# Transposing the attention probabilities as f32 products into both banks of the scores

## The chip, the cores and the metric

The kernel runs on one core of a Trainium2 chip. The metric is the device time of one execution in microseconds. The kernel before takes 629.36 us, the median of three runs (629.0 to 629.54). All times in the sections below come from one profiled execution of it, with 629.1 us and a span of 627.3 us from its first to its last instruction.

## The reference

One layer of a transformer in f32: 16 sequences of 256 tokens with 256 features. Attention has 16 query heads and 4 key and value heads of 128, and a mask that leaves each query the first 4 keys and the last 32. Then follows a feed-forward step whose input and weight are quantised to int8.

```python
x = L0_attn_x                                              # (16, 256, 256)
x = x + attn(layernorm(x), wq, wk, wv, wo)
x = x + ffn(layernorm(x), weight, bias)

# attn
q = (x @ wq.T).reshape(b, t, 16, 128).transpose(0, 2, 1, 3)
k, v = ...                                                  # 4 heads, each used by 4 query heads
scores = einsum('bhtd,bhsd->bhts', q, k_full) / sqrt(128)
mask = (k <= q) & ((k < 4) | (k >= q - 32 + 1))
attn = softmax(scores where mask)
out = einsum('bhts,bhsd->bhtd', attn, v_full) ... @ wo.T

# ffn
w_q, x_q = int8 rounding by row maxima / 127
y = (x_q @ w_q.T) * x_scale * w_scale + bias
```

## The kernel before

The work is cut into 64 units, unit u being batch u // 4 and key head u % 4 with its four query heads. To hold f32 precision with f16 operands, each factor is a high and a low f16 half, and each product is three matmuls (PAIRS). A sequence of 256 queries is cut into 9 steps of 28 or 32 queries with 64 keys each, so a unit's probabilities are PP, 9 tiles of 128 rows (4 heads x 32 queries) by 128 columns (64 keys, high and low half).

The order on each engine is written out by hand, as one loop over turns t = 1 to 60 after a start, and a tail for the last three units. Turn t on TensorE: scores of unit t, PV of unit t - 2 (lines 563 and 564), q fill of unit t + 1 (line 446), a k fill (line 413) or v fill (line 422) for the next batch, then one of these: x's transposes (t mod 4 = 3, line 401), the transposes of quantised x (t mod 4 = 1, line 612), the FFN product (t mod 4 = 2, line 627); then the transposes of the probabilities of unit t - 1 (line 534), and the output projection of unit t - 2 (line 581).

ScalarE in a turn: p_high (line 850), o_high twice (857), q_high (814), exps (821), q_high again, k_high (800 and 801) or v_high (809), x's copy (825) or quantised x's copy (837), and the copy of the transposed probabilities PT (pt_evac, line 830). VectorE: s_max (991, 993), o_low (1007), q_low (983), probs (998 to 1002), q_low, k_low (973) or v_low (978), then by t mod 4 the FFN's steps, among them ffn_norm (1028), and ln_stats (957, 959) of a later batch at t mod 4 = 0. GpSimd: p_low (1320), s_shift (1306), p_norm (1314), and ln_rstd (1288, 1290) at the end of a turn with t mod 4 = 0, ahead of the next turn's p_low. Engines wait for one another by semaphores that count: pt_ok counts the copies of PT, s_m the s_max steps.

PSUM has 8 banks. The scores of a unit lie in banks 2 and 3 (BANK_S). Bank 2 (BANK_PT) also takes the transposed probabilities, as f16 in half of it at a time, and bank 3 (BANK_F) takes x's and quantised x's transposes and the FFN product.

Of the kernel before, what the change touches and what calls it, by code (L numbers as in the profile page):

```python
# [6 lines left out]
F16 = mybir.dt.float16  # L7
# [3 lines left out]
ACT = mybir.ActivationFunctionType  # L11
AX = mybir.AxisListType

B, T, D = 16, 256, 256
# [49 lines left out]
def build(nc, x_d, wq_d, wk_d, wv_d, wo_d, wf_d, bias_d, mask_d, idh_d, idb_d, idf_d, out_d):  # L64
    with ExitStack() as ctx:
# [76 lines left out]
        def half(i, dt):  # L142
            return banks[i].bitcast(dt)
# [125 lines left out]
        def pt_bank(u):  # L269

            return BANK_KV if u in (NU - 4, NU - 3, NU - 1) else BANK_PT
# [72 lines left out]
        def _(pe):  # L344
# [47 lines left out]
            def x_transpose(b):  # L392

                pe.wait_ge(ln_l, b + 1)
                if b:
                    pe.wait_ge(s_m, 1 if b == 1 else 4 * (b - 1))
                v = half(BANK_F, F16).rearrange("p (k l t) -> p k l t", k=2, l=2)
                for k in range(2):
                    for l in range(2):
                        for t in range(2):  # L400
                            a = pe.transpose(v[:, k, l, t * 128:t * 128 + 128], xhl[:, t, l, k * 128:k * 128 + 128], idh[:, :])  # L401
                a.then_inc(xt_ps, 1)
# [94 lines left out]
            def kv_fill(t):  # L497

                b, g = divmod(t, KV)
                if t == 0:  # L500
                    pe.wait_ge(v_l, 1)
                    k_fill(0, 1)
                elif t == 1:
                    pe.wait_ge(xt_ok, 2)
                    pe.wait_ge(k_l, 2)
                    k_fill(1, 0)
                elif t == 2:
                    pe.wait_ge(k_l, 3)
                    v_fill(1, 0)

                    pe.wait_ge(s_m, t + 1)
                    v_fill(1, 1)
                else:
                    if g == 0:
                        pe.wait_ge(xt_ok, b + 2)
                    pe.wait_ge(k_l if g < 2 else v_l, 2 * b + (2, 3, 3, 4)[g])
                    kind, n = KV_TILE[g]
                    (v_fill if kind else k_fill)(b + 1, n)

            def p_transpose(u):  # L520
                p = u % 2
                pe.wait_ge(p_l, u + 1)

                if u == NU - 4:
                    pe.wait_ge(k_l, 2 * B)
                elif u == NU - 3:
                    pe.wait_ge(pt_ok, u)
                elif u == NU - 1:
                    pe.wait_ge(pt_ok, u - 1)
                else:  # L530
                    pe.wait_ge(s_m, u + 2)
                v = half(pt_bank(u), F16).rearrange("p (h q) -> p h q", h=4)
                for s in reversed(range(NT)):
                    a = pe.transpose(v[:, :, STEP * s:STEP * s + 32], PP[:, p, s].rearrange("p l k -> p (l k)"), idh[:, :])  # L534
                a.then_inc(pt_ps, 1)

            def pv(u, j):
                b, g = divmod(u, KV)
                if j == 0:
                    pe.wait_ge(pt_ok, u + 1)  # L540
                    if g == 0 and b < 2:
                        pe.wait_ge(z_ok, 1) if b == 0 else pe.wait_ge(ld_z, 16)
                if g == 0:
                    pe.wait_ge(vw2[j][b % 2], 16 * (b // 2 + 1))
                if u == NU - 3:

                    pe.wait_ge(q_l, 2 * (NU - 1) + j + 1)
                elif u > NU - 3:

                    pe.wait_ge(o_l, 2 * u + j - 3)  # L550
                    if u == NU - 2 and j == 0:
                        pe.wait_ge(f_y, 2 * (B - 2))
                elif u:

                    pe.wait_ge(o_l, 2 * u + j - 1)
                elif j == 0:

                    pe.wait_ge(w_l, l_at("q3"))
                for s, c0, c1 in output_pieces(j):
                    w = max(s - 1, 0)  # L560
                    o = banks[o_bank(u, j)][:, :].rearrange("p (h q) -> p h q", h=4)[:, :, c0 - 128 * j:c1 - 128 * j]
                    pt = PT[:, u % 2].rearrange("p (h q) -> p h q", h=4)[:, :, c0:c1]
                    pe.matmul(o, VW[b % 2][:, w, 0, g * 128:g * 128 + 128], pt, start=True, stop=False)  # L563
                    a = pe.matmul(o, VW[b % 2][:, w, 1, g * 128:g * 128 + 128], pt, start=False, stop=True)  # L564
                a.then_inc(o_ps, 1)
# [36 lines left out]
            def ffn_t(b):  # L602

                pe.wait_ge(f_xq, b + 1)
                if b == B - 2:

                    pe.wait_ge(pt_ok, NU - 1)
                else:
                    pe.wait_ge(s_m, 4 * b + 10)
                for t in range(2):  # L610
                    for k in range(2):
                        a = pe.transpose(xq_view(b, t)[:, k, :], xq[:, t, k * 128:k * 128 + 128], idb[:, :])
                a.then_inc(ft_ps, 1)

            def ffn_mm(b):
                pe.wait_ge(f_t, b + 1)
                if b == 0:
                    pe.wait_ge(wf_s, 14)
                if b < B - 3:

                    pe.wait_ge(s_m, 4 * b + 11)
                elif b == B - 3:

                    pe.wait_ge(o_l, 2 * (NU - 4) + 1)
                for t in range(2):
                    for k in range(2):
                        a = pe.matmul(fm_view(b, t), xqT[:, k, t * 128:t * 128 + 128], WfT[:, k, :], start=(k == 0), stop=(k == 1))  # L627
                a.then_inc(fm_ps, 1)
# [18 lines left out]
            def ffn_weights():  # L647
                v = half(BANK_F, BF16)[:, 0:512].rearrange("p (k o) -> p k o", k=2)
                pe.wait_ge(wf_s, 12)
                pe.wait_ge(ld_idb, 16)  # L650

                pe.wait_ge(s_m, 9)
                for k in range(2):
                    for t in range(2):
                        a = pe.transpose(v[:, k, t * 128:t * 128 + 128], wfi[:, t, k * 128:k * 128 + 128], idb[:, :])
                a.then_inc(wf_ps, 1)

                pe.wait_ge(q_l, 2 * 9 + 1)
                pe.matmul(banks[0][:, 0:256], ones[:, :], diag[:, :, :].rearrange("p t o -> p (t o)"),
                          start=True, stop=True).then_inc(wf_ps, 1)  # L660
# [38 lines left out]
            for t in range(1, NU - 3):  # L699
                b, g = divmod(t, KV)  # L700
                back, more = t > 1, b + 1 < B
                last, mm = at(9, t), at(10, t)
                scores(t)
                if back:
                    pv(t - 2, 0)
                    pv(t - 2, 1)
                q_fill(t + 1, 0)
                q_fill(t + 1, 1)
                if t == 1:
                    columns_up("o")  # L710

                    pe.wait_ge(w_l, l_at("q2"))
                    pe.wait_ge(ld_q[3], 16)
                    w_transpose("q3", big[:, 3, :])
                    maxima_out("o")
                if more:
                    kv_fill(t)
                if g == 3 and b + 2 < B:
                    x_transpose(b + 2)
                if t == 8:  # L720
                    ffn_weights()
                if last is not None:
                    ffn_t(last)
                if mm is not None:
                    ffn_mm(mm)
                p_transpose(t - 1)
                if back:
                    if t == 2:

                        pe.wait_ge(w_s, s_at("o"))  # L730
                    out_proj(t - 2)
                if 1 <= t <= 4:
                    wo_transpose(t - 1)
# [43 lines left out]
        def _(act):  # L777
# [49 lines left out]

            def pt_evac(u):
                act.wait_ge(pt_ps, u + 1)
                act.activation(PT[:, u % 2], half(pt_bank(u), F16), ACT.Copy).then_inc(pt_ok, 1)  # L830

            def ffn_t_evac(b):
                act.wait_ge(ft_ps, b + 1)
# [53 lines left out]
            for t in range(1, NU - 3):  # L887
# [8 lines left out]
                q_high(t + 1, 1)  # L896
                if t == 1:
                    w_high("q3")
                if t == 1:
                    k_high(1, 0)  # L900
                elif t == 2:
                    v_high(1, 0)
                    v_high(1, 1)
                elif more:
                    kind, n = KV_TILE[g]
                    (v_high if kind else k_high)(b + 1, n)
                if g == 3 and b + 2 < B:
                    x_evac(b + 2)
                if last is not None:
                    ffn_t_evac(last)  # L910
                pt_evac(t - 1)
                if t == 2 or (g == 1 and t > 1 and b + 2 < B):
                    ln_split(b + 2)
                if 1 <= t <= 4:
# [520 lines left out]
```

## Time and profile before

| | |
|---|---|
| median of 3 runs | 629.36 us (629.0 to 629.54) |
| profiled execution | 629.1 us, span 627.3 us |
| TensorE busy | 599.1 us, 96% |
| VectorE busy | 542.1 us, 86% |
| ScalarE busy | 399.7 us, 64% |
| GpSimd busy | 314.3 us, 50% |
| mean granted TensorE clock | 0.988 |

TensorE is busy nearly all the time. Its instructions overlap: a matmul's row lasts from its start to its last result, so the cost of a run of matmuls on the engine is read from the start of the run to the start of what follows it. The same holds, by some 0.1 us, for rows of ScalarE and VectorE. PE is TensorE, PEld its weight loads, DVE VectorE, ACT ScalarE, POOL GpSimd.

### The profile page before, as it was taken

The numbers are of one execution on the slowest core, as the hardware profiler recorded it, in microseconds if no ns is written. First come the engines' busy times: TensorE is split into PE (matmuls) and PEld (weight loads), VectorE is DVE, ScalarE is ACT, GpSimd is POOL, SyncE is SP. The second block draws the span as 40 slices with busy tenths as digits, with TensorE's granted clock in tenths as the row PEclk, the third lists the DMA queues.
The fourth block names the chain that finished last, engine by engine and source line by source line (L and its number), as shares of the span: only waits on it lengthen the run. The fifth ranks groups of instructions, "written<-read, shape, count | busy, mean of one in ns | idle before, by whom it ended". The sixth has DMA issues, their size and how long they took to land.

```text
span 627.3 us, 18165 instructions
## 1 busy us (share of the span) xinstructions
PE 599.1 (96%) x7589; PEld 528.9 (84%) x7589; DVE 542.1 (86%) x1083; ACT 399.7 (64%) x632; POOL 314.3 (50%) x310
## 2 busy tenths in 40 slices
PE   5759999999999999999999999999999999999994
PEld 4547888889898888989898898989888898988883
DVE  5876899989888998989898897989899898889886
ACT  5676766566766666667666666766666667666670
POOL 1132445454555646456554645556464545546463
PEclk9989999999999999999999999999999999999997
DMA  8940401213040221304031120304012130402101
GB/s 293 356 108 19 118 1 45 60 28 93 2 119 2 70 51 37 84 6 114 2 93 29 44 77 11 110 2 113 9 51 70 26 95 3 118 2 73 47 12 41
DMA packets 33841, 41.31 MB, mean 66 GB/s; under 512 B 3936, under 2 KB 24416, under 8 KB 33760
## 3 DMA queue, kind: packets, MB, share of 16 engines
q1 hardware_dynamic: 33616, 40.02, 23.0%
q8 instruction: 60, 0.98, 0.7%
q14 instruction: 21, 0.17, 0.1%
q10 hardware_dynamic: 144, 0.13, 0.1%
HBM read 10.26 MB, written 4.19 MB: 23 GB/s over the span
## 4 chain that ended last, share of the span: by engine, by line
PE 88%; DVE 6%; ACT 2%; issue 2%; POOL 1%; DMA 1%; POOLq 0%; SPq 0%; DVEq 0%; ACTq 0%
PE ps L446 25%; PE ps L581 25%; PE ps L476 7%; PE ps L413 7%; PE ps L422 6%; PE ps L534 5%; PE ps L564 4%; PE ps L563 4%; PE ps L401 1%; PE ps L627 1%; PE ps L353 1%; DVE WoT L1121 1%; DMA small<-in_L_attn_wk 1%; PE ps L596 1%; DVE Qs L983 1%
## 5 line engine op out<-in xcount | busy, mean ns | idle before, releaser
L446 PE MATMUL ps<-xT,WqT 128*128 128x256 f16 x1536 | 178.3, 273 | 2.0 <-DVE WqT L1121 1.3
L581 PE MATMUL ps<-WoT,pool 128*128 128x256 f16 x1440 | 167.3, 273 | 0.2 <-DVE pool L1007 0.2
L446 PEld LDWEIGHTS ps<-xT,WqT 128*128 128x128 f16 x1536 | 146.9, 98 | 19.0 <-issue 3.0
L581 PEld LDWEIGHTS ps<-WoT,pool 128*128 128x128 f16 x1440 | 138.2, 98 | 15.3 <-DVE pool L1007 0.3
L1314 POOL TENSOR_TENSOR small<-E,rr 128x576 f32<-128x576 f32 x64 | 73.7, 1152 | 98.4 <-DVE rr L1002 98.4
L857 ACT ACTIVATE pool<-ps 128x512 f16<-128x512 f32 x128 | 69.6, 595 | 81.5 <-PE ps L564 81.4
L1320 POOL TENSOR_TENSOR PP<-small,PP 128x576 f16<-128x576 f32 x64 | 82.2, 1284 | 68.2 <-ACT PP L850 68.2
L814 ACT ACTIVATE Qs<-ps 128x576 f16<-128x576 f32 x128 | 82.5, 644 | 44.9 <-PE ps L446 44.9
L1306 POOL TENSOR_TENSOR Sm<-Sm,mx 128x576 f32<-128x576 f32 x64 | 73.7, 1152 | 53.8 <-DVE mx L993 52.4
L983 DVE TENSOR_TENSOR Qs<-ps,Qs 128x576 f16<-128x576 f32 x128 | 92.6, 724 | 4.7 <-ACT Qs L814 4.7
L1007 DVE SCALAR_TENSOR_TENSOR pool<-ps,pool 128x512 f16<-128x512 f32 x128 | 81.8, 680 | 0.0
L991 DVE TENSOR_TENSOR Sm<-ps,mask 128x576 f32<-128x576 f32 x64 | 47.7, 745 | 27.5 <-PE ps L476 27.5
L830 ACT ACTIVATE PT<-ps 128x1024 f16<-128x1024 f16 x64 | 66.0, 1032 | 6.1 <-PE ps L534 6.1
L821 ACT ACTIVATE E<-Sm,esc 128x576 f32<-128x576 f32 x64 | 49.6, 775 | 28.7 <-POOL Sm L1306 28.7
L998 DVE TENSOR_REDUCE sm<-E 128x9 f32<-128x576 f32 x64 | 48.0, 751 | 18.0 <-ACT E L821 18.0
L476 PE MATMUL ps<-Kw,Qs 128*128 128x64 f16 x1728 | 61.0, 193 | 2.5 <-ACT xT L825 1.4
L476 PEld LDWEIGHTS ps<-Kw,Qs 128*128 128x128 f16 x1728 | 58.7, 98 | 5.2 <-ACT xT L825 1.5
L993 DVE TENSOR_REDUCE mx<-Sm 128x9 f32<-128x576 f32 x64 | 48.2, 754 | 2.2
L413 PE MATMUL ps<-xT,WkT 128*128 128x256 f16 x384 | 49.5, 281 | 0.0
L422 PE MATMUL ps<-WvT,xT 128*128 128x512 f16 x192 | 46.5, 379 | 0.0
L850 ACT ACTIVATE PP<-small 128x576 f16<-128x576 f32 x64 | 43.9, 685 | 2.1 <-POOL small L1314 2.0
L413 PEld LDWEIGHTS ps<-xT,WkT 128*128 128x128 f16 x384 | 38.7, 101 | 5.4
(129 smaller groups left out, 910.3 us busy)
## 6 DMA issues: line engine op xcount, KB each, us to landing
VW<-Vn SPq DMA_DIRECT2D x48, 120.0 KB
big<-Vn SPq DMA_DIRECT2D x48, 120.0 KB
X<-in_L_attn_x SPq DMA_DIRECT2D x16, 256.0 KB, 7.7
VW<-VW SPq DMA_DIRECT2D x16, 256.0 KB, 3.3
big<-big SPq DMA_DIRECT2D x16, 256.0 KB, 3.4
out<-pool SPq DMA_DIRECT2D x15, 256.0 KB, 3.6
big<-in_L_attn_wq SPq DMA_DIRECT2D x4, 512.0 KB, 7.9
pool<-in_L_attn_wo SPq DMA_DIRECT2D x4, 512.0 KB, 9.0
```

Source lines behind the costliest of these rows:

```text
L413: a = pe.matmul(banks[k_bank(b, f)][:, j * 256:j * 256 + 256], WkT[:, k, wl, g * 128:g * 128 + 128], xT[:, b % 2, k, xl, :], start=(n == 1 ...
L422: a = pe.matmul(banks[v_bank(b, t)][:, :], xT[:, b % 2, k, xl, t * 128:t * 128 + 128], WvT[:, k, wl, :], start=(n == 1), stop=(n == 6))
L446: a = pe.matmul(banks[BANK_Q[f]][:, j * 256:j * 256 + 256], WqT[:, k, wl, h * 128:h * 128 + 128], xT[:, b % 2, k, xl, :], start=(n == 1), ...
L476: a = pe.matmul(banks[BANK_S[c]][:, (s - s0) * KEYS:(s - s0 + 1) * KEYS], Qs[:, p, ql, s * 128:s * 128 + 128], Kw[:, b % 2, g, kl, w, :], ...
L581: a = pe.matmul(out_view(b, t), OT[:, p, ol, h, t * 128:t * 128 + 128], WoT[:, 4 * g + h, wl, :], start=first, stop=(end and g == KV - 1), ...
L814: act.activation(dst[0], src, ACT.Copy).then_inc(q_h, 1)
L857: act.activation(OT[:, u % 2, 0, :, cols], src, ACT.Copy, scale=1.0 / P_UP).then_inc(o_h, 1)
L983: dve.tensor_tensor(dst[1], src, dst[0], ALU.subtract).then_inc(q_l, 1)
L1007: dve.scalar_tensor_tensor(OT[:, u % 2, 1, :, cols], src, 1.0 / P_UP, OT[:, u % 2, 0, :, cols], ALU.mult, ALU.subtract).then_inc(o_l, 1)
L1306: pool.tensor_tensor(Sm[:, p], Sm[:, p], mx[:, p, :].unsqueeze(2).to_broadcast([128, NT, KEYS]), ALU.subtract).then_inc(s_d, 1)
L1314: pool.tensor_tensor(Pn[:, p], E[:, p], rr[:, p, :].unsqueeze(2).to_broadcast([128, NT, KEYS]), ALU.mult).then_inc(p_n, 1)
L1320: pool.tensor_tensor(PP[:, p, :, 1, :], Pn[:, p], PP[:, p, :, 0, :], ALU.subtract).then_inc(p_l, 1)
```

## The change

The probabilities of units 0 to 59 are no longer transposed by 9 PE transposes of 128 columns to f16, but by 10 ordinary products with columns of the identity, which write f32: 128 columns for the first piece, 48 and 64 where a step crosses the middle of the sequence, and 112 (4 heads x 28 queries) otherwise. The result takes 1024 f32 columns, that is both banks of the scores. ScalarE's copy reads both banks, and PT is laid out half by half instead of head by head.

Since bank 3 now holds the transposed probabilities too, the order changes: on TensorE the probabilities come right after the q fill, ahead of the k or v fill, and x's transposes, quantised x's transposes, the FFN product and a v fill of the start follow them and wait for pt_ok in place of s_m. On ScalarE the copy of PT comes right after the second q_high. The four last units keep the old form.

```diff
@@ -393,7 +393,7 @@
 
                 pe.wait_ge(ln_l, b + 1)
                 if b:
-                    pe.wait_ge(s_m, 1 if b == 1 else 4 * (b - 1))
+                    pe.wait_ge(s_m, 1) if b == 1 else pe.wait_ge(pt_ok, 4 * (b - 1) - 1)
                 v = half(BANK_F, F16).rearrange("p (k l t) -> p k l t", k=2, l=2)
                 for k in range(2):
                     for l in range(2):
@@ -508,7 +508,7 @@
                     pe.wait_ge(k_l, 3)
                     v_fill(1, 0)
 
-                    pe.wait_ge(s_m, t + 1)
+                    pe.wait_ge(pt_ok, t)
                     v_fill(1, 1)
                 else:
                     if g == 0:
@@ -529,6 +529,17 @@
                     pe.wait_ge(pt_ok, u - 1)
                 else:
                     pe.wait_ge(s_m, u + 2)
+                if u < NU - 4:
+
+                    eye = idh[:, :].rearrange("p (h q) -> p h q", h=4)
+                    for j in range(2):
+                        v = banks[BANK_S[j]][:, :].rearrange("p (h q) -> p h q", h=4)
+                        for s, c0, c1 in output_pieces(j):
+                            i = c0 - STEP * s
+                            a = pe.matmul(v[:, :, c0 - 128 * j:c1 - 128 * j], PP[:, p, s].rearrange("p l k -> p (l k)"),
+                                          eye[:, :, i:i + c1 - c0], start=True, stop=True)
+                    a.then_inc(pt_ps, 1)
+                    return
                 v = half(pt_bank(u), F16).rearrange("p (h q) -> p h q", h=4)
                 for s in reversed(range(NT)):
                     a = pe.transpose(v[:, :, STEP * s:STEP * s + 32], PP[:, p, s].rearrange("p l k -> p (l k)"), idh[:, :])
@@ -559,7 +570,7 @@
                 for s, c0, c1 in output_pieces(j):
                     w = max(s - 1, 0)
                     o = banks[o_bank(u, j)][:, :].rearrange("p (h q) -> p h q", h=4)[:, :, c0 - 128 * j:c1 - 128 * j]
-                    pt = PT[:, u % 2].rearrange("p (h q) -> p h q", h=4)[:, :, c0:c1]
+                    pt = PT[:, u % 2, 512 * j:512 * j + 512].rearrange("p (h q) -> p h q", h=4)[:, :, c0 - 128 * j:c1 - 128 * j]
                     pe.matmul(o, VW[b % 2][:, w, 0, g * 128:g * 128 + 128], pt, start=True, stop=False)
                     a = pe.matmul(o, VW[b % 2][:, w, 1, g * 128:g * 128 + 128], pt, start=False, stop=True)
                 a.then_inc(o_ps, 1)
@@ -605,8 +616,10 @@
                 if b == B - 2:
 
                     pe.wait_ge(pt_ok, NU - 1)
+                elif b == B - 3:
+                    pe.wait_ge(s_m, 4 * b + 10)
                 else:
-                    pe.wait_ge(s_m, 4 * b + 10)
+                    pe.wait_ge(pt_ok, 4 * b + 9)
                 for t in range(2):
                     for k in range(2):
                         a = pe.transpose(xq_view(b, t)[:, k, :], xq[:, t, k * 128:k * 128 + 128], idb[:, :])
@@ -618,7 +631,7 @@
                     pe.wait_ge(wf_s, 14)
                 if b < B - 3:
 
-                    pe.wait_ge(s_m, 4 * b + 11)
+                    pe.wait_ge(pt_ok, 4 * b + 10)
                 elif b == B - 3:
 
                     pe.wait_ge(o_l, 2 * (NU - 4) + 1)
@@ -649,7 +662,7 @@
                 pe.wait_ge(wf_s, 12)
                 pe.wait_ge(ld_idb, 16)
 
-                pe.wait_ge(s_m, 9)
+                pe.wait_ge(pt_ok, 8)
                 for k in range(2):
                     for t in range(2):
                         a = pe.transpose(v[:, k, t * 128:t * 128 + 128], wfi[:, t, k * 128:k * 128 + 128], idb[:, :])
@@ -713,6 +726,7 @@
                     pe.wait_ge(ld_q[3], 16)
                     w_transpose("q3", big[:, 3, :])
                     maxima_out("o")
+                p_transpose(t - 1)
                 if more:
                     kv_fill(t)
                 if g == 3 and b + 2 < B:
@@ -723,7 +737,6 @@
                     ffn_t(last)
                 if mm is not None:
                     ffn_mm(mm)
-                p_transpose(t - 1)
                 if back:
                     if t == 2:
 
@@ -827,7 +840,11 @@
 
             def pt_evac(u):
                 act.wait_ge(pt_ps, u + 1)
-                act.activation(PT[:, u % 2], half(pt_bank(u), F16), ACT.Copy).then_inc(pt_ok, 1)
+                if u < NU - 4:
+                    src = ps[:, BANK_S[0]:BANK_S[1] + 1, :].rearrange("p j (h q) -> p j h q", h=4)
+                else:
+                    src = half(pt_bank(u), F16).rearrange("p (h j q) -> p j h q", h=4, j=2)
+                act.activation(PT[:, u % 2].rearrange("p (j h q) -> p j h q", j=2, h=4), src, ACT.Copy).then_inc(pt_ok, 1)
 
             def ffn_t_evac(b):
                 act.wait_ge(ft_ps, b + 1)
@@ -896,6 +913,7 @@
                 q_high(t + 1, 1)
                 if t == 1:
                     w_high("q3")
+                pt_evac(t - 1)
                 if t == 1:
                     k_high(1, 0)
                 elif t == 2:
@@ -908,7 +926,6 @@
                     x_evac(b + 2)
                 if last is not None:
                     ffn_t_evac(last)
-                pt_evac(t - 1)
                 if t == 2 or (g == 1 and t > 1 and b + 2 < B):
                     ln_split(b + 2)
                 if 1 <= t <= 4:
```

On TensorE, turn 9 (t mod 4 = 1) of the kernel before, from the q fill to the output projection. xq is quantised x, xT x transposed; the brackets name the semaphores that a row waits for.

```order
L446 MATMUL ps<-xT,WqT 128x256 [waits wf_s,q_l]
L446 MATMUL ps<-xT,WqT 128x256 x11
L446 MATMUL ps<-xT,WqT 128x256 [waits q_l]
L446 MATMUL ps<-xT,WqT 128x256 x11
L422 MATMUL ps<-WvT,xT 128x512 [waits k_l]
L422 MATMUL ps<-WvT,xT 128x512 x5
L612 MATMUL ps<-idb,xq 128x128 [waits s_m,f_xq]
L612 MATMUL ps<-idb,xq 128x128 x3
L534 MATMUL ps<-idh,PP 128x4x32 [waits s_m,p_l]
L534 MATMUL ps<-idh,PP 128x4x32 x8
L581 MATMUL ps<-WoT,pool 128x256 [waits o_l]
```

The same turn on TensorE in the changed kernel, where line 539 holds the new products, 625 quantised x's transposes and 592 the output projection.

```order
L446 MATMUL ps<-xT,WqT 128x256 x11
L539 MATMUL ps<-idh,PP 128x4x32 [waits s_m,p_l]
L539 MATMUL ps<-idh,PP 128x4x28 x3
L539 MATMUL ps<-idh,PP 128x4x12
L539 MATMUL ps<-idh,PP 128x4x16
L539 MATMUL ps<-idh,PP 128x4x28 x4
L422 MATMUL ps<-WvT,xT 128x512 [waits k_l]
L422 MATMUL ps<-WvT,xT 128x512 x5
L625 MATMUL ps<-idb,xq 128x128 [waits pt_ok,f_xq]
L625 MATMUL ps<-idb,xq 128x128 x3
L592 MATMUL ps<-WoT,pool 128x256 [waits o_l]
```

The probabilities have moved ahead of the v fill, and quantised x's transposes behind them, now with a wait for the copy of PT.

On ScalarE, the same turn before, from exps to p_high of the next turn.

```order
L821 ACTIVATE E<-Sm,esc 128x576 [waits s_d]
L814 ACTIVATE Qs<-ps 128x2x9x32 [waits q_ps]
L809 ACTIVATE Vn<-ps 128x512 [waits vw10,vw00,v_ps]
L837 ACTIVATE xqT<-ps 128x512 [waits ft_ps]
L830 ACTIVATE PT<-ps 128x1024 [waits pt_ps]
L795 ACTIVATE xhl<-xn 128x2x256 [waits xt_ps,ln_xn]
L850 ACTIVATE PP<-small 128x9x64 [waits pt_ps,p_n]
```

And now:

```order
L834 ACTIVATE E<-Sm,esc 128x576 [waits s_d]
L827 ACTIVATE Qs<-ps 128x2x9x32 [waits q_ps]
L847 ACTIVATE PT<-ps 128x1024 [waits pt_ps]
L822 ACTIVATE Vn<-ps 128x512 [waits vw10,vw00,v_ps]
L854 ACTIVATE xqT<-ps 128x512 [waits ft_ps]
L808 ACTIVATE xhl<-xn 128x2x256 [waits xt_ps,ln_xn]
L867 ACTIVATE PP<-small 128x9x64 [waits pt_ps,p_n]
```

The copy of PT has moved from behind quantised x's copy to right behind the second q_high. VectorE's and GpSimd's orders are unchanged.

## Rows read from the trace of the kernel before

**Rows 1.** The page, busy us, share of the span and instructions.
```profile
PE 599.1 (96%) x7589; PEld 528.9 (84%) x7589; DVE 542.1 (86%) x1083; ACT 399.7 (64%) x632; POOL 314.3 (50%) x310
```

**Rows 2.** Stretches: busy us and count of each engine, granted clock, DMA share, GB/s.
```profile
40.00:50.00 10.00, 5.24 (x38) 4.24 (x36) 4.75 (x13) 4.12 (x9) 3.53 (x3) 0.66 0.35 91
...
200.00:500.00 300.00, 300.00 (x3912) 267.19 (x3910) 265.48 (x524) 195.15 (x308) 163.47 (x159) 1.00 0.20 51
```

**Rows 3.** TensorE's timeline: start us, us, line, operation, tiles; turns 31 to 34.
```profile
319.31 2.78 PE L446 MATMUL ps<-xT,WqT 128*128 128x256 f16 x24
...
331.12 1.47 PE L413 MATMUL ps<-xT,WkT 128*128 128x256 f16 x12
...
337.25 2.78 PE L446 MATMUL ps<-xT,WqT 128*128 128x256 f16 x24
339.87 1.46 PE L422 MATMUL ps<-WvT,xT 128*128 128x512 f16 x6
341.17 0.39 PE L612 MATMUL ps<-idb,xq 128*128 128x128 bf16 x4
341.39 0.67 PE L534 MATMUL ps<-idh,PP 128*128 128x128 f16 x9
341.89 2.78 PE L581 MATMUL ps<-WoT,pool 128*128 128x256 f16 x24
344.51 0.95 PE L476 MATMUL ps<-Kw,Qs 128*128 128x64 f16 x27
...
345.30 0.22 PE L563 MATMUL ps<-PT,VW 128*128 128x128 f16 x1
...
346.21 2.02 PE L446 MATMUL ps<-xT,WqT 128*128 128x256 f16 x17
```

**Rows 4.** ScalarE's timeline: exps in three turns, and what follows it.
```profile
321.41 0.78 ACT L821 ACTIVATE E<-Sm,esc 128x576 f32<-128x576 f32 x1
...
331.21 0.78 ACT L821 ACTIVATE E<-Sm,esc 128x576 f32<-128x576 f32 x1 [0.54 <-POOL Sm L1306]
...
340.54 0.78 ACT L821 ACTIVATE E<-Sm,esc 128x576 f32<-128x576 f32 x1 [1.13 <-POOL Sm L1306]
341.22 0.63 ACT L814 ACTIVATE Qs<-ps 128x576 f16<-128x576 f32 x1
341.75 0.58 ACT L809 ACTIVATE Vn<-ps 128x512 f16<-128x512 f32 x1
```

**Rows 5.** Timelines near 50 us: a copy of PT, and the matmul that it releases.
```profile
49.93 1.03 ACT L830 ACTIVATE PT<-ps 128x1024 f16<-128x1024 f16 x1
...
51.10 0.95 PE L476 MATMUL ps<-Kw,Qs 128*128 128x64 f16 x27 [0.61 <-ACT PT L830]
```

**Rows 6.** ScalarE's timeline: k_high in a turn with t mod 4 = 0.
```profile
332.63 0.97 ACT L800 ACTIVATE Kw<-ps 128x960 f16<-128x960 f32 x1
333.50 0.22 ACT L801 ACTIVATE Kw<-ps 128x64 f16<-128x64 f32 x1
```

**Rows 7.** VectorE's timeline: s_max and k_low of that turn, the end of ln_stats.
```profile
328.42 0.74 DVE L991 TENSOR_TENSOR Sm<-ps,mask 128x576 f32<-128x576 f32 x1
...
333.75 1.15 DVE L973 TENSOR_TENSOR Kw<-ps,Kw 128x960 f16<-128x960 f32 x1
...
336.92 0.18 DVE L959 BATCH_NORM_AGGREGATE mv<-st 128x2 f32<-128x6 f32 x1
```

**Rows 8.** GpSimd's timeline after it: ln_rstd, p_low, s_shift.
```profile
337.18 0.20 POOL L1288 TENSOR_TENSOR rs<-mv,cst 128x2 f32<-128x2 f32 x1 [2.73 <-DVE mv L959]
...
338.12 1.27 POOL L1320 TENSOR_TENSOR PP<-small,PP 128x576 f16<-128x576 f32 x1
339.35 1.15 POOL L1306 TENSOR_TENSOR Sm<-Sm,mx 128x576 f32<-128x576 f32 x1
```

**Rows 9.** Timelines near 579 us: VectorE's ffn_norm beside GpSimd's p_low.
```profile
578.47 1.73 DVE L1028 TENSOR_SCALAR pool<-X,mv,rs 128x256 f32<-128x256 f32 x2
...
578.77 1.28 POOL L1320 TENSOR_TENSOR PP<-small,PP 128x576 f16<-128x576 f32 x1 [0.79 <-ACT PP L850]
```

## The prediction

> **What bounds the kernel now.** I read the page's busy line first [rows 1], then the stretches [rows 2], TensorE's timeline through a turn, and the other engines' timelines over the same time. TensorE is busy 599.1 of 627.3 us, and in the stretch from 200 to 500 us it is busy 300.00 of 300.00 us at a granted clock of 1.00 (2.4 GHz) [rows 1, 2]. There every turn is a gapless chain of matmuls, so a column saved on TensorE is time saved, and a wait put into its queue is time lost in full. One turn with t mod 4 = 1 goes, from the q fill at 337.25 to the next at 346.21, in 8.96 us: q fill, v fill at +2.62, transposes of quantised x at +3.92, of the probabilities (PP) at +4.14, output projection at +4.64, PV at +8.05 [rows 3]. A v or k fill takes 1.30 us (339.87 to 341.17). All offsets below count from the turn's q fill. Four turns are one batch; I call a turn with t mod 4 = 1 kind 1, and so on. Kind 1 holds the transposes of quantised x, 2 the FFN product, 3 x's transposes, 0 none of these.
>
> **What the change saves.** The 9 transposes of PP take 0.50 us (341.39 to 341.89 [rows 3]). In their place stand 10 products with 4 x 128, 112, 112, 112, 48, 64 and 4 times 112 columns, the shapes of the PV loop, whose 20 products of just these widths take 346.21 - 345.30 = 0.91 us [rows 3], so 10 take 0.455: 0.045 us saved in each of 60 turns, 2.7 us in all. A product of new kind (identity as moving operand with stride, f32 out) isn't in the trace; the bounds: 10 products at 29 ns, the pace of the scores' 27 products of 64 columns (345.30 - 344.51 = 0.79 us [rows 3]), would take 0.29 us, and at the pace of the old ones, 56 ns, 0.56. That is 12.6 us saved to 3.6 lost over 60 turns; I take PV's pace, the nearest row. The Trainium skill ("TensorE: Matmul & The Clock Gate", LDWEIGHTS) has a rule against the change: a weight load takes its columns at 1.2 GHz, 107 ns for 128. By it ten loads would cost 107 ns more per turn than nine, about 6 us in 60 turns. The trace doesn't agree, since the scores load 128 columns for each product and start one every 29 ns, so I leave it out of the sum.
>
> ScalarE's copy of the transposed probabilities reads the same 1024 elements, now f32 over two banks. I keep the 1.03 us of today's copy [rows 5].
>
> **What the change adds: a wait for ScalarE.** The products fill both banks of the scores, and the second is the one in which x's and quantised x's transposes and the FFN product land. So these now wait until ScalarE has copied PT out (pt_ok), where before they waited for VectorE's s_max, long past. Behind that wait stand, on TensorE's in-order queue, the output projection, the next scores and PV: nothing can fill it. When is PT copied? TensorE issues: q fill to 2.62, products to 3.075, k or v fill to 4.375. At 4.375 it wants the shared bank.
>
> ScalarE's order is q_high, exps, q_high, then now the copy. After exps starts, the second q_high starts 0.68 later and the next instruction 0.53 after that (340.54, 341.22, 341.75 [rows 4]), and the copy takes 1.03: done 2.24 us after exps' start. A matmul freed by ScalarE starts 0.14 us after the end of what it waited for: 51.10 against 49.93 + 1.03 [rows 5].
> - Kinds 2 and 3: exps starts at 321.41 in a turn of kind 3 whose q fill starts at 319.31, +2.10 [rows 3, 4]; kind 2 is alike. The second q_high can't start before its products end (+2.82), so the copy runs from 3.35 to 4.38, and the matmul starts at 4.52. Loss 0.145, less 0.045: +0.10 each.
> - Kind 0: nothing waits. -0.045.
> - Kind 1: exps starts at 340.54, +3.29 [rows 4]. With that alone the copy ends at 5.53 and the wait ends at 5.67: 1.29 us lost.
>
> But exps comes later still. It is held by GpSimd: s_shift stands behind p_low, and that behind ln_rstd, which waits for VectorE's last ln_stats instruction (336.92 + 0.18, and then 337.18, 338.12, 339.35) [rows 7, 8]. VectorE runs without a gap there, from k_low at 333.75 [rows 7]. k_low started just when ScalarE's two k_high ended (333.50 + 0.22 [rows 6]). In the changed kernel the k fill comes after the products, 0.455 us later, and k_high with it (332.63 is 0.04 after the k fill's last matmul, 331.12 + 1.47 [rows 3, 6]). So k_low and ln_stats end 0.455 us later, while that turn, of kind 0, itself is 0.045 shorter: exps in the next turn starts at 3.29 + 0.50 = 3.79. Copy from 5.00 to 6.03, transposes of quantised x at 6.17. The rest of the turn is 8.96 - 3.92 less the PP transposes' 0.50, 4.54 us: 10.71 against 8.96, +1.75. (p_low also ends 0.50 later, 2.64 instead of 2.14 [rows 8], and then holds the products some 0.15 us; it doesn't count, since q_high holds the copy longer.)
>
> After that wait VectorE and ScalarE have slack again and kind 2 starts as before, so the loss comes once a batch: 1.75 + 0.10 + 0.10 - 0.045 = +1.9 us.
>
> **Sum.** 12 full turns of kind 1 (t = 9 to 53): 21.0. 13 FFN products and 13 x transposes in the steady part: 2.6. 14 turns of kind 0: -0.6. Turn 57 (no ln_stats before it) and turns 1 to 6 (a v fill and x's transposes wait likewise, but the PT copy comes sooner in the first turn): +1.1, between -1 and +4. The tail keeps the old path. +24.1 us against the profiled run's 629.1, which is 0.3 under the median of 629.36: 653.5.
>
> **Rivals.**
> - VectorE is caught by GpSimd's p_low. In kind 3 VectorE's two ffn_norm instructions (L1028) now start 0.25 later and p_low (L1320) 0.45 earlier, as p_high no longer queues behind the PT copy; the second L1028 would start within 0.05 us of p_low. At 578.47 the trace shows what follows when p_low is first: the pair takes 1.73 us, until p_low's end at 578.77 + 1.28 [rows 9], not 0.72 as in an undisturbed turn. That would move s_max of kind 0 from -0.08 (328.42 [rows 7], q fill 331.12 - 2.62) to about +0.37; exps, today at 331.21 [rows 4], goes with it, so does the copy, now ahead of k_high, and k_low starts 1.15 later than before instead of 0.455. Another 0.69 us in each of 12 turns: 661.8. For it: p_low came 0.02 us before the second L1028's turn there, and they nearly tie here. Against it: by my chaining VectorE is first by 0.04. The Trainium skill ("SBUF — State Buffer", SBUF: two separate sides) says the same of the port pair that both share: whichever starts first holds it for the whole instruction.
> - exps doesn't move, because VectorE makes up the 0.455 in kind 0: 1.29 - 0.045 instead of 1.75 per such turn, 12 x 0.5 less: 647.5. Against it: k_low to ln_stats has no gap.
> - TensorE's clock falls after its new pauses. It fell to 0.66 in the stretch from 40 to 50 us, with TensorE busy 5.24 of 10 us [rows 2]. If 5 us after each of 12 pauses ran at 1.2 GHz, 2.5 us would be lost each time: 683. Against it: the new pause is 1.8 us, and there TensorE stood over 4.
> - Not slower: the copy of PT in kind 1 starts before 3.2, so that no wait shows. Place: ScalarE's exps, which would have to start at +2.0 instead of +3.8. Then only savings are left, 629.1 - 2.7 = 626.4. With exps at +2.1 in all turns the waits of 0.145 stay: 3 waits less 0.18, +0.25 per batch, 632.5. Against both: ln_rstd's wait for VectorE.
> - The products don't pay: at 56 ns each another 6.3 us on the forecast, at 29 ns 9.9 less. They shift the time within its range.
>
> **How the numbers follow.** Forecast (653.5) 0.48; p_low first (661.8) 0.27; exps unmoved (647.5) 0.12; clock 0.04; waits of 0.145 only 0.04; not slower 0.05. Within 0.2% is about what a measurement of this kernel can tell from no change. Faster 0.03, same 0.02, slower 0.95. The range, 645 to 665, takes in the first three with about 2 to 3 us for the size of the small terms; some 15 in 100 are left out.
>
> **What would show it.** TensorE's waits in the changed profile list the transposes of quantised x behind ScalarE's PT copy, about 13 times and near 1.8 us each, some 20 us in all, with x's transposes and the FFN product at 0.1 to 0.2. Exps in kind 1 starts near +3.8 (+4.5 if the first rival holds, and L1028 of kind 3 then takes about 1.7 us as a pair). The ten products take 0.455 us. TensorE's clock stays 1.00 between 200 and 500 us. The forecast is wrong if the transposes of quantised x follow the v fill without a gap, or if PT's copy is much longer than 1.03 us from f32.

## The result and the profile after

The changed kernel takes 664.99 us (median of 4 runs, 664.84 to 665.77) against 629.31 us for the kernel before on the same chip: 1.0568 times as long, 95% interval 1.0555 to 1.058. Forecast were 653.5 us; the median lies on the upper edge of the range of 645 to 665, and two of the four runs lie above it. The sign was right, and so was the wait for the shared bank, but not its size. The second most likely case, in which GpSimd's p_low catches VectorE (661.8 us), is what happened, with first turns dearer than I had priced.

The page after [rows 1]: TensorE has some 6 us more to do by its rows and is busy for a smaller share.

```profile
PE 604.9 (91%) x7649; PEld 523.1 (79%) x7649; DVE 551.1 (83%) x1083; ACT 400.9 (60%) x632; POOL 314.3 (47%) x310
```

Three of the changed kernel's waits, in the order of their totals: who waited for whom, us in total, times, longest. None of these three TensorE waits stood in the kernel before.

```profile
PE ps L625 <- ACT PT L847: 19.3, 13, 1.5
...
PEld ps L539 <- POOL PP L1337: 10.3, 11, 0.9
...
PE ps L539 <- POOL PP L1337: 7.2, 11, 0.7
```

Line 625 holds quantised x's transposes, 13 times, as forecast. The 7.2 us are not in the forecast, which put at 0.15 us what p_low holds the products: they wait for it 11 times, up to 0.7 us.

Stretches of one batch, turns 29 to 32, one row for each turn (kinds 1, 2, 3, 0), then of the long middle [rows 2].

```profile
317.63:329.07 11.44, 9.24 (x120) 7.50 (x117) 8.07 (x18) 6.25 (x11) 5.68 (x6) 1.00 0.01 1
329.07:338.35 9.28, 9.28 (x120) 7.75 (x117) 8.17 (x18) 5.25 (x9) 4.80 (x6) 1.00 0.09 18
338.35:347.63 9.28, 9.28 (x129) 8.38 (x126) 8.81 (x14) 6.52 (x11) 6.84 (x6) 1.00 0.45 129
347.63:356.33 8.70, 8.70 (x121) 8.03 (x119) 7.67 (x18) 5.62 (x10) 2.30 (x2) 1.00 0.26 64
```

```profile
200.00:500.00 300.00, 282.45 (x3653) 244.63 (x3650) 253.27 (x490) 183.24 (x287) 153.45 (x149) 1.00 0.18 48
```

(The first row's turn is one of kind 1; the trace before has 8.96, 9.17, 9.19 and 8.75 us for the four kinds.) Kind 1 carries the loss, 2.48 us a batch; kinds 2 and 3 lose 0.11 and 0.09, kind 0 wins 0.05. The clock stayed at 1.00.

TensorE through that turn of kind 1, which answers to [rows 3].

```profile
317.63 2.78 PE L446 MATMUL ps<-xT,WqT 128*128 128x256 f16 x24
321.07 0.63 PE L539 MATMUL ps<-idh,PP 128*128 128x128 f16 x10 [0.66 <-POOL PP L1337]
321.54 1.46 PE L422 MATMUL ps<-WvT,xT 128*128 128x512 f16 x6
324.53 0.38 PE L625 MATMUL ps<-idb,xq 128*128 128x128 bf16 x4 [1.53 <-ACT PT L847]
324.75 2.78 PE L592 MATMUL ps<-WoT,pool 128*128 128x256 f16 x24
```

The products start at +3.44 instead of +2.62, where the q fill is issued, and quantised x's transposes at +6.90 instead of +3.92 [rows 3]. An undisturbed run of the ten products is in the turn after: 331.69 to 332.14.

```profile
331.69 0.62 PE L539 MATMUL ps<-idh,PP 128*128 128x128 f16 x10
332.14 1.46 PE L422 MATMUL ps<-WvT,xT 128*128 128x512 f16 x6
```

That is 0.45 us, the price taken from PV. ScalarE in the turn of kind 1 [rows 4]:

```profile
322.16 0.77 ACT L834 ACTIVATE E<-Sm,esc 128x576 f32<-128x576 f32 x1 [2.37 <-POOL Sm L1323]
322.84 0.63 ACT L827 ACTIVATE Qs<-ps 128x576 f16<-128x576 f32 x1
323.37 1.01 ACT L847 ACTIVATE PT<-ps 128x1024 f16<-128x1024 f32 x1
```

Exps starts at +4.53, against +3.29 before and +3.79 forecast; the copy follows 1.21 behind, takes 1.01 us from f32, and the transposes start 0.15 after its end. The chain from exps to the wait is as worked out; exps itself is late by 0.74 more. Where from, VectorE and GpSimd show, from kind 3 on (q fill at 338.35) [rows 7 to 9].

```profile
344.05 1.16 DVE L990 TENSOR_TENSOR Kw<-ps,Kw 128x960 f16<-128x960 f32 x1 [0.17 <-ACT Kw L814]
...
345.25 1.75 DVE L1045 TENSOR_SCALAR pool<-X,mv,rs 128x256 f32<-128x256 f32 x2
...
348.05 0.73 DVE L1008 TENSOR_TENSOR Sm<-ps,mask 128x576 f32<-128x576 f32 x1
...
354.07 1.16 DVE L990 TENSOR_TENSOR Kw<-ps,Kw 128x960 f16<-128x960 f32 x1 [0.61 <-ACT Kw L814]
...
357.24 0.18 DVE L976 BATCH_NORM_AGGREGATE mv<-st 128x2 f32<-128x6 f32 x1
```

```profile
345.58 1.28 POOL L1337 TENSOR_TENSOR PP<-small,PP 128x576 f16<-128x576 f32 x1 [1.08 <-ACT PP L867]
...
357.50 0.20 POOL L1305 TENSOR_TENSOR rs<-mv,cst 128x2 f32<-128x2 f32 x1 [3.42 <-DVE mv L976]
...
358.44 1.28 POOL L1337 TENSOR_TENSOR PP<-small,PP 128x576 f16<-128x576 f32 x1
```

K_low of kind 3 starts at +5.70, 0.25 us later than before, as worked out. Then the pair of ffn_norm takes 1.75 us instead of 0.72, the collision of the first rival: p_low starts 0.33 after the pair's start, while its second instruction would start 0.32 after the first, as in an undisturbed pair. S_max of kind 0 comes at +0.42 (347.63 is the q fill), k_low at +6.44 instead of +5.25, ln_stats ends at +1.09 into the next turn instead of -0.15, and p_low behind it.

### The profile page after: what moved, and what is told of

The parts are those of the page before. It is cut to its first block, busy times and chain, and to the rows that moved or that the text cites. A ratio compares the mean times of both kernels' runs of the same rounds, so it can differ in the third digit from the quotient of the medians.

```text
span 664.0 us, 18285 instructions
## 1 busy us (share of the span) xinstructions
PE 604.9 (91%) x7649; PEld 523.1 (79%) x7649; DVE 551.1 (83%) x1083; ACT 400.9 (60%) x632; POOL 314.3 (47%) x310
## 4 chain that ended last, share of the span: by engine, by line
PE 43%; issue 16%; ACT 16%; POOL 13%; DVE 11%; DMA 1%; POOLq 0%; SPq 0%; ACTq 0%; DVEq 0%
PE ps L592 12%; PE ps L446 11%; POOL Sm L1323 5%; POOL PP L1337 5%; PE ps L476 3%; PE ps L413 3%; ACT Kw L813 3%; PE ps L422 3%; ACT PT L847 3%; ACT E L834 2%; PE ps L539 2%; PE ps L575 2%; PE ps L574 2%; ACT PP L867 2%; ACT Qs L827 2%
## 5 line engine op out<-in xcount | busy, mean ns | idle before, releaser
L592 PEld LDWEIGHTS ps<-WoT,pool 128*128 128x128 f16 x1440 | 139.6, 98 | 17.1 <-DVE pool L1024 0.7
L847 ACT ACTIVATE PT<-ps 128x1024 f16<-128x1024 f32 (+1 forms) x64 | 65.0, 1016 | 3.8 <-PE ps L539 2.2
L990 DVE TENSOR_TENSOR Kw<-ps,Kw 128x960 f16<-128x960 f32 x32 | 37.0, 1157 | 15.3 <-ACT Kw L814 15.2
```

Of the source, the lines that this page charges most:

```text
L592: a = pe.matmul(out_view(b, t), OT[:, p, ol, h, t * 128:t * 128 + 128], WoT[:, 4 * g + h, wl, :], start=first, stop=(end and g == KV - 1), ...
L847: act.activation(PT[:, u % 2].rearrange("p (j h q) -> p j h q", j=2, h=4), src, ACT.Copy).then_inc(pt_ok, 1)
```

## The experiments

The theory (A): in kind 1 TensorE waits for ScalarE's copy of PT at the shared bank; the copy stands behind exps, exps behind ln_rstd and p_low on GpSimd, and these behind ln_stats, which the new order and the collision make late. Rivals: the products' form costs, the order alone costs, the collision only passes its time on. Turn lengths, in us, from q fill to q fill in turns 33 to 36 of each profile:

| kernel | median us | kind 1 | kind 2 | kind 3 | kind 0 |
|---|---|---|---|---|---|
| before | 629.3 | 8.96 | 9.17 | 9.20 | 8.75 |
| changed | 664.99 | 11.44 | 9.28 | 9.29 | 8.70 |
| order alone | 642.21 | 9.87 | 9.17 | 9.20 | 8.75 |
| old products, new order and waits | 665.93 | 11.44 | 9.28 | 9.29 | 8.75 |
| kind 1 in the old form | 648.89 | 9.79 | 9.68 | 9.29 | 8.70 |
| ffn_norm ahead of k_low | 666.65 | 11.59 | 9.28 | 9.29 | 8.70 |
| p_low waits for ffn_norm | 657.23 | 10.87 | 9.28 | 9.29 | 8.70 |
| ln_stats ahead of k_low | 659.43 | 11.00 | 9.28 | 9.29 | 8.70 |
| copy of PT ahead of exps | 653.61 | 9.80 | 9.93 | 9.29 | 8.70 |
| products into PV's banks | 626.72 | 8.91 | 9.12 | 9.15 | 8.70 |

**The order alone.** The kernel before, with the calls moved as in the change:

```diff
+                p_transpose(t - 1)
                 if more:
                     kv_fill(t)
...
                     ffn_mm(mm)
-                p_transpose(t - 1)
```

with pt_evac(t - 1) moved likewise on ScalarE.

> The kernel before with the changed order alone: the 9 f16 transposes of the probabilities come right after the q fill, ScalarE's copy of PT right after the second q_high; they stay in bank 2, and nothing new waits for pt_ok. Theory A (the loss is the shared bank plus a later exps): kinds 2, 3 and 0 as before; kind 1 loses what p_low comes late, some 0.8 us where VectorE is caught by p_low, in 11 or 12 turns: about 638 us. Theory B (only the wait on the shared bank costs): 629. Theory C (the order alone makes the loss, the bank nothing): 660 or more.

Measured: 642.21 us, 1.0209 times before (1.0195 to 1.0223). Kinds 2, 3 and 0 are unchanged, kind 1 loses 0.91, all of it ahead of the transposes:

```profile
347.75 0.68 PE L534 MATMUL ps<-idh,PP 128*128 128x128 f16 x9 [0.74 <-POOL PP L1320]
348.27 1.46 PE L422 MATMUL ps<-WvT,xT 128*128 128x512 f16 x6
349.56 0.39 PE L612 MATMUL ps<-idb,xq 128*128 128x128 bf16 x4
```

The collision is here too, two turns earlier:

```profile
333.24 1.75 DVE L1028 TENSOR_SCALAR pool<-X,mv,rs 128x256 f32<-128x256 f32 x2
```

So 13 of the 35.7 us come with the order, through p_low, without any shared bank; the other 23 with the waits. Theories B and C both fall. Theory A was 4 us too low: kind 1 loses 0.91 and not 0.8, and turns 8 and 9 lose 0.73 and 1.05. How much of the 13 us is the collision's, this run doesn't show.

**The form alone.** The changed kernel with `if u < 0:` in place of `if u < NU - 4:` in p_transpose and pt_evac, so that all units are transposed by 9 f16 transposes.

> The changed kernel, order and waits kept, but the old 9 transposes to f16 in bank 2 for all units: what the form of the products is worth by itself. Theory A: 60 turns x (0.50 - 0.455) us = 2.7 us more than the changed kernel, 667.7. If f32 products or the f32 copy are what costs, it is faster than 664.99 by more than 1 us.

Measured: 665.93 us, 1.0585 times before (1.057 to 1.0599), an interval that overlaps that of the changed kernel. The 2.7 us of the expectation were wrong: the products' 0.05 us show in kind 0 alone (8.75 against 8.70). In the other kinds the wait for the copy ends when it did, and swallows them. That the form costs is ruled out.

**Kind 1 in the old form.**

```diff
-                if u < NU - 4:
+                if u < NU - 4 and u % 4:
...
-                elif b == B - 3:
+                else:
                     pe.wait_ge(s_m, 4 * b + 10)
-                else:
-                    pe.wait_ge(pt_ok, 4 * b + 9)
```

and the same condition `u % 4` in pt_evac.

> The changed kernel, but units 0, 4, 8, ... (whose probabilities are transposed in turns of kind 1) keep the f16 transposes in bank 2, so quantised x's transposes wait for s_m again and not for the copy of PT. Order unchanged. Theory A: kind 1 falls from 11.44 us to about 9.8 (0.8 of waiting for p_low stays), 11 turns x 1.66 and 1 us more: 645.7. If something else than that wait holds TensorE, it stays above 655.

Measured: 648.89 us (1.0314, 1.0299 to 1.0328). Kind 1 is 9.79 as worked out, so the wait on the bank is what it cost. The total is 3 us above the 645.7 worked out: kind 2, which I had left alone, loses 0.40 in each of 11 turns, 4.4 us, while turns 9 and 57 win 2.6, where 1 was put in.

```profile
358.37 2.78 PE L446 MATMUL ps<-xT,WqT 128*128 128x256 f16 x24
...
363.30 0.60 PE L638 MATMUL ps<-WfT,xqT 128*128 128x256 bf16 x4 [0.40 <-ACT PT L845]
```

```profile
360.93 0.78 ACT L832 ACTIVATE E<-Sm,esc 128x576 f32<-128x576 f32 x1 [0.40 <-POOL Sm L1321]
```

Without the long pause of kind 1 the other engines enter kind 2 late, exps starts at +2.56 instead of +2.10, and the FFN product waits for the copy instead.

**ffn_norm ahead of k_low.** On VectorE, at t mod 4 = 3:

```diff
                 elif more:
+                    if norm is not None:
+                        ffn_norm(norm)
                     kind, n = KV_TILE[g]
                     (v_low if kind else k_low)(b + 1, n)
...
-                if norm is not None:
+                if norm is not None and not more:
                     ffn_norm(norm)
```

> The changed kernel, but VectorE does ffn_norm ahead of k_low in kind 3, so that its two tensor_scalar are done long before GpSimd's p_low starts. Theory A with the collision: ln_stats ends 0.7 us earlier in the next turn, kind 1 falls from 11.44 to 10.7, 11 times: 657. If the collision is harmless: 665.

Measured: 666.65 us (1.0596, 1.0581 to 1.061), a miss. The experiment didn't take the collision away, it made two others:

```profile
343.73 1.18 DVE L1045 TENSOR_SCALAR pool<-X,mv,rs 128x256 f32<-128x256 f32 x2
344.94 0.69 DVE L1048 TENSOR_REDUCE fx<-pool 128x2 f32<-128x512 f32 x1
345.66 1.16 DVE L1050 TENSOR_SCALAR fx<-fx 128x2 f32<-128x2 f32 x1
```

```profile
343.28 1.15 POOL L1333 TENSOR_TENSOR small<-E,rr 128x576 f32<-128x576 f32 x1 [0.36 <-DVE rr L1019]
...
345.51 1.28 POOL L1339 TENSOR_TENSOR PP<-small,PP 128x576 f16<-128x576 f32 x1 [1.08 <-ACT PP L867]
```

The pair starts inside p_norm and takes 0.46 us more; the small tensor_scalar starts inside p_low (345.51 to 346.79) and ends with it, 1.16 us for two elements. S_max of kind 0 comes at +0.56. So this run says nothing against the collision's price, and the next one was made to take the collision away.

**p_low waits for ffn_norm.** On GpSimd:

```diff
+                if at(7, t - 1) is not None:
+                    pool.wait_ge(f_xn, 2 * at(7, t - 1) + 2)
                 p_low(t - 1)
```

> The changed kernel, but GpSimd's p_low in turns of kind 0 first waits for both instructions of ffn_norm, so it can't fall between them. Theory A with the collision: the pair takes 0.72 us instead of 1.75; ffn_norm's small tensor_scalar is then held by p_low instead, as in the kernel before, so s_max of kind 0 comes 0.6 us earlier, k_low is held by k_high alone and ln_stats ends 0.7 us earlier: kind 1 falls from 11.44 to about 10.7, 11 times, 657. Rival: the collision's time is only passed on, as when ffn_norm was put ahead of k_low: 665.

Measured: 657.23 us (1.0445, 1.0428 to 1.0463), 7.8 us under the changed kernel, by a wait added.

```profile
341.09 0.73 DVE L1045 TENSOR_SCALAR pool<-X,mv,rs 128x256 f32<-128x256 f32 x2
...
342.57 0.63 DVE L1050 TENSOR_SCALAR fx<-fx 128x2 f32<-128x2 f32 x1
```

```profile
341.90 1.28 POOL L1337 TENSOR_TENSOR PP<-small,PP 128x576 f16<-128x576 f32 x1 [1.57 <-DVE pool L1045]
```

The pair is back at 0.73 us and kind 1 at 10.87, near the 10.71 of the forecast. The small tensor_scalar is held by p_low instead (0.63 us), as expected. The collision was worth 0.57 us in each of 11 turns of kind 1, 6.3 us in all, and about as much in each of turns 8, 57 and 60, while turn 9 loses 0.13. The rival, 665, falls. This is the kernel that the forecast described, and it still takes 3.7 us more than the 653.5 forecast.

**ln_stats ahead of k_low**, at t mod 4 = 0 on VectorE:

```diff
+                    if g == 0 and b + 2 < B:
+                        ln_stats(b + 2)
                     kind, n = KV_TILE[g]
                     (v_low if kind else k_low)(b + 1, n)
...
-                if g == 0 and b + 2 < B:
-                    ln_stats(b + 2)
```

> The changed kernel, but VectorE does ln_stats ahead of k_low in kind 0. Theory A: exps of kind 1 stands behind ln_rstd, and that behind ln_stats. p_low then ends before TensorE wants the products (the 0.66 us wait goes), and s_shift is held by s_max instead, with exps some 0.3 us earlier, if p_low doesn't catch quantised x's rounding on VectorE: kind 1 about 11.1, 661. Rival, exps isn't held by ln_rstd: 665.

Measured: 659.43 us (1.0478, 1.0462 to 1.0494). Exps of kind 1 was held by p_low behind ln_rstd: now that it isn't, TensorE gets the products at once (355.40, +2.62) and exps starts at +4.10 instead of +4.53.

```profile
352.08 1.62 DVE L1057 TENSOR_SCALAR xr<-pool,fx 128x256 f32<-128x256 f32 x2
...
354.07 0.75 DVE L1008 TENSOR_TENSOR Sm<-ps,mask 128x576 f32<-128x576 f32 x1
```

```profile
352.01 1.28 POOL L1337 TENSOR_TENSOR PP<-small,PP 128x576 f16<-128x576 f32 x1
```

But p_low comes early enough to catch the rounding of x (1.62 instead of 0.61 us), which delays s_max, and exps with it: one wait is traded for another.

**Copy of PT ahead of exps**, in kind 1 on ScalarE: q_high, q_high, pt_evac, exps.

> The changed kernel, but in turns of kind 1 from turn 5 on ScalarE does both q_high, then the copy of PT, then exps. Theory A: the copy no longer stands behind exps; it ends at about +5.1 instead of +6.75, quantised x's transposes at +5.3 instead of +6.9, kind 1 at about 9.8 instead of 11.44: 647. If TensorE is held by p_low or by the later exps: above 655.

Measured: 653.61 us (1.0389, 1.0375 to 1.0404). Kind 1 falls to 9.80, as expected, but the total is 6.6 us above the 647 expected: 0.65 comes back in each of 12 turns of kind 2, again at the FFN product, and 1.3 in turn 6.

```profile
354.54 0.63 PE L539 MATMUL ps<-idh,PP 128*128 128x128 f16 x10 [0.65 <-POOL PP L1343]
...
356.37 0.38 PE L625 MATMUL ps<-idb,xq 128*128 128x128 bf16 x4
...
366.09 0.60 PE L640 MATMUL ps<-WfT,xqT 128*128 128x256 bf16 x4 [0.65 <-ACT PT L847]
```

**Products into PV's banks.** The kernel before with its old order; units 1 to 59 use the ten products, but write the banks of PV (4 and 5), which the last o_low has just left and which PV of the same unit writes next.

```diff
+                if 0 < u < NU - 4:
+                    pe.wait_ge(o_l, 2 * u)
+                    ...
+                        v = banks[BANK_O[j]][:, :].rearrange("p (h q) -> p h q", h=4)
```

> The kernel before, old order, but units 1 to 59 are transposed by the 10 f32 products, into PV's two banks (4 and 5) instead of the scores': free there since the last o_low, and written again only by PV of the same unit, which needs PT anyway. No new wait on ScalarE for x's and quantised x's transposes. Theory A: only the savings are left, 59 x 0.045 = 2.7 us, 626.7 and faster than both kernels. If the products' form costs something of its own: 629.4 or more.

Measured: 626.72 us (626.57 to 626.83, 5 runs) against 628.93, ratio 0.9961 (0.9947 to 0.9974): faster than both kernels. Each turn is 0.05 us shorter than before (8.91 against 8.96 in kind 1), which is what the form saves; the gain of 2.2 us lies by its interval between 1.6 and 3.3, with the expected 2.7 inside.

```profile
338.19 1.46 PE L422 MATMUL ps<-WvT,xT 128*128 128x512 f16 x6
339.49 0.39 PE L623 MATMUL ps<-idb,xq 128*128 128x128 bf16 x4
339.71 0.62 PE L539 MATMUL ps<-idh,PP 128*128 128x128 f16 x10
340.16 2.78 PE L592 MATMUL ps<-WoT,pool 128*128 128x256 f16 x24
```

No gap anywhere in the turn, and the products take 0.45 us. So f32 products into two banks were never the trouble; the choice of banks was, with the new order and the waits that it brings. This run keeps the old order too, so it doesn't part the two; the run with the order alone does.

## Why the prediction was wrong

The parts that held. TensorE was gapless, and a wait there counted in full. The products took 0.45 us (0.455 taken), the copy from f32 1.01 (1.03). Kinds 2, 3 and 0 changed by +0.11, +0.09 and -0.05 (+0.10, +0.10, -0.045). In kind 1 the wait sat where it was put, 1.21 + 1.01 + 0.15 us after exps' start. The clock didn't fall, and exps did move, so those two rivals are out. When the collision was taken away, kind 1 measured 10.87 (10.71), the small rest because k_high in kind 0 stood behind the copy for 0.17 us. (Among the widths of the ten products the working has "4 x 128"; it is one piece of 128 columns, 4 x 32, and the sum of 1024 columns is right.)

The step that failed is the choice between the forecast and its first rival: "by my chaining VectorE is first by 0.04". The measured starts stand 0.01 us apart, and the second ffn_norm was held until p_low's end. Two times chained over five instructions each are not known to 0.04 us; I had priced the rival nearly rightly (10.71 + 0.69 = 11.40 for kind 1, 11.44 measured) and should have read the near tie as open. Worse, the trace had shown the outcome of a near tie, at 578.47 [rows 9], and it went this way. Kind 1 came out 0.73 above the forecast, in 11 turns 8.0 of the 11.5 us by which the forecast was short. By the run with the wait added, 0.57 of the 0.73 is the collision, 6.3 us; the other 0.16 is k_high behind the copy, which the forecast had not seen and which stays without the collision.

The rest is in the first turns and turn 57. For the term "Turn 57 [...] and turns 1 to 6", +1.1, turn lengths give +1.4 for turns 1 to 6 and +1.37 for turn 57. Turn 7 lost 1.46 and turn 8 lost 0.84, where the forecast had +0.10 and -0.045, while turn 9 lost 1.23 and not 1.75. In turn 7 x's transposes wait, and in turn 8 those of the FFN weights, a part of the diff that I did not price:

```profile
110.31 0.61 PE L401 MATMUL ps<-idh,xhl 128*128 128x128 f16 x8 [1.35 <-ACT PT L847]
...
120.34 0.38 PE L668 MATMUL ps<-idb,wfi 128*128 128x128 bf16 x4 [0.72 <-ACT PT L847]
```

I had put turn 7 into the steady part, but its exps starts at +3.53 (107.94 after 104.41), not at +2.10, since VectorE rounds the FFN weights just ahead of s_max; in the kernel before it stood at +3.22 there already. The profile of the changed kernel also starts its turns 0.8 us later than that of the kernel before. The ten profiles differ in this by up to 1.2 us, and no run shows why, so it stays out of this account.

## What to carry to other kernels

Before a result is moved to a larger or another piece of PSUM, list for each bank who writes it next and whose release that writer then waits for. A bank that its own consumer will write anyway (here PV's) added no wait; one shared with a stage of other timing made TensorE wait for the end of a chain on three other engines. Where two engines' starts come out within some hundredths of a microsecond in a forecast, both outcomes should be given like chances, and an experiment that moves one instruction must be read for new collisions before it is taken as a test. A pause on the busiest engine gives the others slack; take it out, and part comes back in the next turn (0.40 and 0.65 us here).

## What the runs showed of the hardware

- In these traces VectorE's tensor_scalar on SBUF data, of two elements a partition or more, didn't run beside a GpSimd tensor_tensor that had started before it: it waited for the end of it. Two elements took 1.16 us, until p_low's end; the ffn_norm pair took 1.75 us when p_low started within it, 1.18 when it started within p_norm, and 0.73 alone. Adding one semaphore wait on GpSimd won 7.8 us. A tensor_scalar of a single element was not held: in the kernel before it takes its usual 0.20 us, from 8.55 us on, in the middle of GpSimd's row from 7.94 to 9.09. The Trainium skill ("SBUF — State Buffer", SBUF: two separate sides) describes an exclusive lock on a port pair that both engines share, held for the whole instruction by whichever starts first; of VectorE's instructions it names those in a 2-port perf mode and those with two SBUF inputs. The traces agree on the lock; in which mode a tensor_scalar ran, they don't show.
- A product with strided columns of the identity costs TensorE what PV's products of the same widths cost: ten with 1024 columns in all take 0.45 us, against 0.50 us for nine transposes of 128.
- ScalarE copies 1024 f32 elements from two banks in 1.01 to 1.03 us, as long as 1024 f16 elements from one.
